# Identity products carried on into batch 0, and GpSimd's wait for x moved behind the lead

## The reference

```python
qkv = x @ W_qkv
q, k, v = heads(split(qkv))                      # 16 heads, 8 channels each
scores = einsum('bhnd,bhmd->bhnm', q, k) / sqrt(128.0)
attn = softmax(scores, axis=-1)
out = einsum('bhnm,bhmd->bhnd', attn, v)
x = layernorm(x + out)                           # then the experts, layer 1, ...
```

## Time and profile before

| | |
|---|---|
| median of 3 runs | 1274.61 us (1269.41 to 1274.92) |
| the profiled execution's own time | 1271.47 us |
| its span | 1269.6 us |
| mean granted TensorE clock | 0.782 |
| busy: PE, DVE, ACT, POOL | 95%, 66%, 58%, 35% |

### The profile page before, as it was taken

The page is one execution under the profiler, slowest core; times in us unless marked ns, Lnnn a source line. Parts: engine busy times, 40 slices in busy tenths (PEclk is TensorE's granted clock), DMA queues, the critical chain, the costliest instruction groups (busy, mean ns, idle before and its releaser), DMA issues. The chain is left out here.

```text
span 1269.6 us, 20149 instructions
## 1 busy us (share of the span) xinstructions
PE 1210.9 (95%) x5827; PEld 559.5 (44%) x5827; DVE 836.7 (66%) x1870; ACT 730.6 (58%) x933; POOL 444.6 (35%) x427
## 2 busy tenths in 40 slices
PE   8999999999999999999999999999999999999997
PEld 3332322323232232322478888887843332232285
DVE  6745556555555555555788877889976666663477
ACT  1144444444444444445765555555678888889954
POOL 1110110202011020350367766777773333330065
PEclk9855555555555555555999999999999999999999
DMA  5522011110111112000034433333335222232001
GB/s 164 194 100 66 21 50 48 62 46 14 67 42 50 46 38 63 13 2 2 20 126 126 135 123 121 112 108 102 132 119 174 82 80 88 74 96 78 1 18 51
DMA packets 68085, 97.00 MB, mean 76 GB/s; under 512 B 11896, under 2 KB 30328, under 8 KB 67648
## 3 DMA queue, kind: packets, MB, share of 16 engines
q1 hardware_dynamic: 68032, 96.35, 23.8%
HBM read 67.98 MB, written 27.79 MB: 75 GB/s over the span
## 5 line engine op out<-in xcount | busy, mean ns | idle before, releaser
L770 DVE TENSOR_REDUCE a_nmax<-a_ps_f 128x1 f32<-128x512 f32 x512 | 322.0, 683 | 240.5 <-PE a_ps_f L611 240.5
L535 ACT ACTIVATE a_prob<-a_ps_s 128x1024 f32<-128x1024 f32 x256 | 251.9, 1023 | 255.7 <-PE a_ps_s L678 255.7
L1398 ACT ACTIVATE a_prob<-a_ps_s 128x1024 f32<-128x1024 f32 x256 | 244.5, 1026 | 27.8 <-PE a_ps_s L1450 26.8
L611 PE MATMUL a_ps_f<-a_ks,a_qs 24*128 24x512 f32 x512 | 215.0, 757 | 24.2 <-DVE a_nmax L770 22.8
L691 PE MATMUL a_ps_o<-a_prob,a_va 128*32 128x512 f32 x1024 | 236.4, 1015 | 0.3 <-ACT a_prob L535 0.3
L611 PEld LDWEIGHTS a_ps_f<-a_ks,a_qs 24*128 24x128 f32 x512 | 81.3, 271 | 290.7 <-DVE a_nmax L770 232.3
L2218 POOL TENSOR_TENSOR moe_hl<-moe_hid,moe_hh 128x512 fp32r<-128x512 f32 x134 | 174.2, 1305 | 84.1 <-ACT moe_hh L2099 84.0
L678 PE MATMUL a_ps_s<-a_qs,a_ks 26*128 26x512 f32 x512 | 194.6, 662 | 1.3 <-ACT a_prob L535 1.2
L2089 ACT ACTIVATE moe_ps<-moe_ps 128x512 f32<-128x512 f32 x128 | 74.5, 582 | 111.6 <-PE moe_ps L2012 110.8
L1463 PE MATMUL a_ps_o<-a_prob,a_va 128*32 128x512 f32 x1024 | 136.4, 605 | 1.7 <-DVE a_turned_o L1578 1.2
L839 POOL TENSOR_TENSOR a_msplit<-a_nmax,g_zero 128x32 fp32r<-128x32 f32 x16 | 3.8, 239 | 298.5 <-DVE a_nmax L770 298.5
(11 more groups left out here) (308 smaller groups left out, 1651.4 us busy)
## 6 DMA issues: line engine op xcount, KB each, us to landing
moe_cw<-r_weights SPq DMA_DIRECT2D x256, 128.0 KB, 2.8
parts_q<-a_parts SPq DMA_DIRECT2D x32, 256.0 KB, 2.6
parts_k<-a_parts SPq DMA_DIRECT2D x24, 256.0 KB, 2.5
a_qs<-parts_q SPq DMA_DIRECT2D x64, 96.0 KB, 2.4
a_ks<-parts_k SPq DMA_DIRECT2D x64, 96.0 KB, 2.5
a_qs<-parts_q SPq DMA_DIRECT2D x124, 48.0 KB
a_ks<-parts_k SPq DMA_DIRECT2D x124, 48.0 KB
parts_q<-a_parts SPq DMA_DIRECT2D x8, 512.0 KB, 2.8
```

The source lines that it names most:

```text
L535: nc.scalar.activation(prob[:, u % PSLOTS, :, :], ps_s[:, u % 2, :, :], ACT.Exp, scale=float(P) ** -0.5).then_inc(exp_done, 1)
L611: nc.tensor.matmul(ps_f[:, bank, :], quarter_rows(qs[p], h, FQKR)[:, qt * P:(qt + 1) * P], quarter_rows(ks[p], h, FQKR), start=True, stop= ...
L770: nc.vector.tensor_reduce(nmax[:, half_no, h % HG, col:col + 1], ps_f[:, bank, :], AX.X, ALU.max, negate=True).then_inc(max_done, 1)
L1398: nc.scalar.activation(prob[:, u % PSLOTS, :, :], ps_s[:, u % 2, :, :], ACT.Sigmoid, scale=float(HD) ** -0.5).then_inc(exp_done, 1)
```

## The change

Two edits, both in `attention0`. On TensorE, three identity products are also issued at the end of each of batch 0's first three units (units 0, 1 and 2), nine products in all. On GpSimd, the wait for `x_in` moves from ahead of the lead to behind the lead's last piece of work, `split_max(0, 0)`.

```diff
@@ constants
 WARM = (5, 2, 3)
+FIRST_PV = 3
@@ TensorE's units
-                    if not back and 2 * u >= LATE:
+                    if not back and 2 * u >= LATE or is_first(b) and u < FIRST_PV:
                         warm_up(WARM[2])
@@ GpSimd's units
                     split_max(b + 1, 0)
+                    if isinstance(b, int) and b < 0:
+                        pool.wait_ge(x_in, 16)
@@ GpSimd's program
-            pool.wait_ge(x_in, 16)
             walk(pool, units)
```

## The result

| | before | changed |
|---|---|---|
| median | 1273.07 us (1269.41 to 1274.92, 4 runs) | 1259.81 us (1254.44 to 1260.49, 4 runs) |
| profiled execution's span | 1269.6 us | 1257.3 us |
| mean granted clock | 0.782 | 0.795 |

The ratio is 0.989, with a 95% interval of 0.9853 to 0.9927: 13 us faster where 9 were forecast (1265.5 us, range 1250 to 1275). In later runs both kernels spread more: the changed one took 1245.4 to 1267.9 us in twelve executions, and four executions of the kernel before took 1147 to 1181. On the chip that ran the twelve, the medians were 1263.8 and 1268.4 us, 4.6 apart. The spread is itself a finding; the experiments show where most of it comes from.

What follows compares the result with a forecast made beforehand. TensorE, 95% busy, ran layer 0's attention at half clock. Lead 5.4, trios -1.3, full clock up to `q` 8.8, wait for batch 2's x -3.8: 9.1 us saved, 1265.5 us forecast, range 1250 to 1275.

Steps and rivals of the forecast that it cites:

- GpSimd's wait: Layer 0's attention lead: moving the wait splits the maxima by 36.3 and removes TensorE's 2.2 us gap, saving 5.4 us.
- The nine products: Batch 0's first three units: the identity trios cost 1.3 us (bounds nothing and 3.8); first V product at 55.4.
- The pair at full clock: Pair of units in layer 0's attention: 4.16 us at half clock becomes about 2.67, no less than 2.5.
- What is late next: Batch 2's `q` product: TensorE waits some 3.8 us for x, which lands at 73.4, and loses the clock.
- The rest of the stage: Behind `q`: half clock in the same order as before, with the 9.1 us gained at `q` kept.
- the clock is lost for good at `q`: After the wait for batch 2's x at `q`, the clock stays at 0.50 until 600.
- the clock coming back: Rival for layer 0's attention: the clock comes back or never falls, kept for the whole stage; 1082 us, chance 0.08.
- the wait's move does nothing: Rival: another wait holds GpSimd as long; gain about 7 us, 1267.6, if the clock holds; 0.10 including other small outcomes.

Runs made afterwards that it cites:

- e1: Changed kernel without the nine identity products, only GpSimd's moved wait; 1259.2 us (1173.8 to 1267.4, 6 runs), kernel before 1268.1.
- e7: The changed kernel run again, on the same chip as the denser-mix runs; 1263.8 us (1245.4 to 1267.9, 12 runs), kernel before 1268.4.
- e5: Changed kernel with batch 2's x loaded early and one identity product ahead of every odd unit's scores; 1107.0 us (1086.4 to 1141.4, 6 runs).
- e11: Changed kernel with two identity products in every odd unit and batch 2's x loaded behind maximum rows and stack reads; 1112.1 us, kernel before 1269.9.
- e3: Changed kernel with batch 2's x loaded ahead of the weight loads; 1230.8 us (1182.5 to 1267.9, 6 runs), kernel before 1268.1.
- e2: Changed kernel with GpSimd's wait put back, only the nine identity products; 1260.0 us over six executions, one of them 1626.6, kernel before 1268.1.
- e6: Changed kernel with two identity products in every odd unit, batch 2's x loaded where the changed kernel does; 1102.3 us (1101.5 to 1104.5, 4 runs).
- e8: Kernel before with two identity products in every odd unit and neither edit; 1105.2 us (1103.9 to 1111.3, 4 runs), kernel before 1269.9.
- e9: Kernel before with GpSimd's moved wait and two identity products in every odd unit, without the nine; 1101.6 us (4 runs), kernel before 1269.9.

## Why the prediction was right

**GpSimd's wait.** Right. The gap went, the lead stayed at 1.00. The lead's gain is 5.0 us where 5.4 were forecast: first `s2` 51.43 for 55.72, with the whole lead starting 0.7 us later in this profile (the VectorE run of 31.96 in the earlier trace rows starts at 32.64).

**The nine products.** They cost 0.9 us (first `s2` to first V product 4.73 for 3.83) where I took 1.3, and the clock stayed up to `q`; e1's profile, without them, lost it in the first V group.

**The pair at full clock.** Forecast 2.67 us from latencies of other stages, measured 2.70. TensorE was ready for `q` 14.6 us after the first V product (forecast 14.2), at 70.75.

**What is late next.** The right transfer, the right cause; the size was off. The wait is 1.89 us and not 3.8: TensorE came 1.1 us later than forecast, and the load was issued 0.7 us sooner, since the last weight load landed 6.9 us after its issue and not 9.2. And since the clock fell only near 73.5, the `q` product itself still ran at full clock, 1.18 us for 2.08, a term that I had left out. The gain at the k product, which starts at 92.86 in the kernel before, is 92.86 - 82.07 = 10.8 us, for 9.1 forecast at `q`:

```profile
92.86 2.08 PE L601 MATMUL a_ps_f<-a_xt,a_w 128*128 128x512 f32 x2
```

**The rest of the stage.** The shift stays at 10.8 us through the batches (474.04 to 463.27 at the last k product). Another 1.6 us came where I had nothing: in the last batch the clock returned at 585.6 and not at 601.2. The windows, first the kernel before and then the changed one:

```profile
601.00:602.00 1.00, 1.00 (x12) 0.16 (x8) 1.00 (x2) 0.57 (x1) 0.00 (x0) 0.88 0.00 0
585.60:586.60 1.00, 1.00 (x13) 0.49 (x13) 0.00 (x0) 0.35 (x2) 0.00 (x0) 1.00 0.00 0
```

That is chance as far as the runs show: e1's profile has the return near 560, e7's, which is the changed kernel again, at 593.6. Together 12.4, against 12.3 between the spans. The median is luckier than the steps: 13 us in four runs of each, 4.6 in the later twelve and eighteen, where five executions of the kernel before lie under 1256 us.

**Where my reasoning was wrong** is the step "the clock is lost for good at `q`", as a statement on the clock, and with it the 0.08 for the clock coming back. It was lost in the changed kernel's profile, for 512 us. But the kernel before has executions at 1147 to 1181 us, whose mean granted clocks of 0.868 to 0.902 leave 225 to 311 us at half clock where most have some 550; e5 regained it after 133 us, and e11 within 9 us. I had read 517 us at 0.50 with TensorE 95% busy as if that row settled it, and it is one execution. The comparison with layer 1 was off too: at full clock TensorE is busy for 2.89 or 3.04 of 3.40 us in this mix (e3, e2), and for 152 of 160 us in layer 1's attention, so the mix that kept the clock was the denser one. I weighed the Trainium skill's "TensorE: Matmul & The Clock Gate", section "What's actually happening" (activity releases the slow clock), against the rows and gave it little. e11, with its clock back in 9 us, agrees with it; the 510 us at 0.50 with TensorE busy for 485 don't, if activity is read as busy share. The Trainium skill's section "HAM oscillation — how this bites in real kernels", on the same page, tells of waits for a DMA that send the clock back to half. The loss at `q` agrees, though the waits in the section's example are longer than the 1.89 us here; the losses in e2 and e3, where no wait is over 0.4 us, it does not cover.

Nor did I see that moving GpSimd's wait makes the stall at `q` that the trios alone don't have (e2), although the rival "the wait's move does nothing" had the two numbers, TensorE at 75.1 and x at 75.5. By times the two edits alone (1259.2 and 1260.0, before 1268.1) can't be told from both together (1263.8, before 1268.4).

## What to carry to other kernels

Read the clock row before the busy row: a stage that is 95% busy at half clock is bound by the clock, and its busy share says nothing of what it could do. Here a few products of the full array, put where TensorE waits anyway, made the stage half as fast again (a pair in 2.76 us for 4.16) for nearly nothing. Put them through the whole stage and not only at its entry: a stall of 6 us then cost 10 and not the stage. That full width is what counts was not tested; no run used narrow products as filling. And when one queue's wait is removed, look for who now arrives earlier than the transfer it needs.

## What the runs showed of the hardware

At the same instruction stream the clock of such a stage differs from execution to execution, and the time with it: 1147 to 1278 us for the kernel before, 1182 to 1268 with x early, 1086 to 1141 with one product a pair (the mean granted clock goes from 0.776 to 0.902, 0.785 to 0.864 and 0.939 to 0.998). With two and both edits it is 1101 to 1104. A short stall is one way to lose it: stalls of 1.89 and 2.11 us came with the loss in the two profiles of the changed kernel. It doesn't decide alone: stalls of 0.41, 1.18 and 1.37 us left the clock at 1.00 in e6, e8 and e9, where the mix is dense, and in e2 and e3 it fell inside steady pairs of 2.70 us with TensorE busy for 3.04 of 3.40 and 2.89 of 3.40 us. What makes a mix dense enough, the width of the products or their number, wasn't measured.
